# First graph attention of a two-layer kernel: the mask is brought into PSUM once for two heads, the odd head's logits come from a difference added to the same bank, and there are four logit buffers in place of three

## The chip, the cores and the metric

The program runs on one core of one Trainium2 chip. The metric is the device time of that core in microseconds, the median of several executions. The kernel before takes 2636.36 us (three runs, 2636.29 to 2637.47).

## What is computed

The whole program is two layers, each an attention over a graph of 2708 nodes with 256 features, followed by a feed-forward part. The change touches the first attention alone, whose reference is, cut to what matters:

```python
support = (inputs @ weight).reshape(n, H, OUT_F).transpose(1, 0, 2)      # H = 4 heads of 64
f1 = jnp.einsum('hno,ho->hn', support, weight_u[..., 0])
f2 = jnp.einsum('hno,ho->hn', support, weight_v[..., 0])
logits = f1[:, None, :] + f2[:, :, None]
w = jax.nn.leaky_relu(logits, NEG_SLOPE)
masked = w * adj_mat
mask = adj_mat != 0.0
neg = jnp.where(mask, masked, -jnp.inf)
m = jnp.max(neg, axis=2, keepdims=True)
e = jnp.where(mask, jnp.exp(neg - m), 0.0)
denom = jnp.sum(e, axis=2, keepdims=True)
out = jnp.einsum('hnm,hmo->hno', e / denom, support)
```

The rows of an output tile are 128 nodes, so there are 22 tiles; a row of logits has 2708 columns. The mask is the same for the four heads of a tile.

## The kernel before, in words

`layer0_attention` works in units. A unit is one tile and one head (22 x 4 = 88 units); a pair is the two units of heads 0 and 1, or 2 and 3, of one tile (44 pairs). In the names of the trace `a_` stands ahead of the tiles of this stage. The five engines run their own programs, written out without loops over the units by `over_units`, which calls a function `step` of each engine once per unit; the order within an engine is the order of the code, and semaphores tie the engines together. A unit "of an even head" is head 0 or 2.

A unit passes through these places:
- TensorE, `logits(unit, c)`: a row of logits comes in three chunks of 1024, 1024 and 660 columns. For each chunk, one of two PSUM slots `fo` gets the mask (OFF through the identity IDB, line 770) and then the logits (ROWS and FP, line 772), each as matmuls of at most 512 columns. It may write a slot when VectorE has read the chunk two places before (`leaky_done`).
- VectorE, `leaky(unit, c)` (line 683) makes the leaky value of a chunk out of `fo` into the logit buffer `lg`; `mask(unit)` (line 691) multiplies the whole row with ADJ and takes the maximum, and line 694 negates it.
- ScalarE, `exp_part(unit)` (line 626): the exponential of a whole row with its sum.
- TensorE, `turn` (line 785): 22 transposes of 128x128 blocks into three PSUM banks `tp`, four blocks to a bank, so six groups: groups 0 to 2 first and 3 to 5 (10 blocks) later in the step.
- ScalarE, `copies` (line 570): each group is copied from `tp` into `wt`. `copied` lets TensorE use the bank again.
- TensorE, `weighted(pair, half)` (line 800): the product with V, both heads of a pair side by side, in two halves of 11 blocks each, one half in each step of the pair two units later. `heads_in` is raised by the second half. `po` has one place for the sums, so half 0 waits for `heads_out` of the pair before.
- ScalarE, `sums_out` (line 634) copies the sums into `ot`; TensorE, `turn_back` (line 808), turns them; VectorE, `finish` (line 714), adds them to X and raises `heads_out`.

TensorE's step for a unit is: groups 0 to 2 of this unit, the third chunk of logits of the unit two later, groups 3 to 5, in a step of an even head `turn_back`, two chunks of logits of the unit three later, half of `weighted`. ScalarE's step is: copies of groups 0 to 2, in a step of an even head `sums_out` of the pair before last, the exponential of the next unit, copies of groups 3 to 5. VectorE's step is: three `leaky` of the unit two later, in a step of an even head `finish`, in one of head 3 `row_stats`, then `mask` of the unit two later, and in a step of an odd head `reciprocals`.

`copies` waits, besides for the transposes, for `heads_in` of the pair two before the unit's own, since `wt` holds two pairs:

```python
if first_of(unit).later(-4):
    eng.wait_ge(heads_in, pairs(first_of(unit).later(-4)))
copy(wt[:, h // 2, h % 2, j:end, :], tp[:, BANKS[g], 0:(end - j) * P]).then_inc(copied[BANKS[g]], 1)
```

(`later(k)` counts in units, so `later(-4)` of the first unit of a pair is the pair two before; `pairs` turns a pair into the count that its semaphore has.)

Of the kernel before, what the change touches and what calls it, by code (L numbers as in the profile page):

```python
# [5 lines left out]
ALU = mybir.AluOpType  # L6
# [8 lines left out]
P = 128  # L15
# [145 lines left out]
def layer0_prepare(nc, io, keep):  # L161
# [4 lines left out]
    with Phase(nc, "p0") as ph:  # L166
# [106 lines left out]
        def _(dve):  # L273
# [28 lines left out]
            def selectors():  # L302
# [6 lines left out]
                dve.wait_ge(sel_done, 3)  # L309
                for h in range(H):  # L310
                    dve.tensor_scalar(SEL[:, h, :], ones[:, :], hsel[:, h:h + 1], None, ALU.mult).then_inc(sel_done, 1)

            def first_rows(b):

                dve.wait_ge(sel_done, 3 + H)
                dve.tensor_copy(ROWS[:, b, :, :], SEL[:, :, :]).then_inc(sel_done, 1)
# [156 lines left out]
LB = 3  # L473
# [3 lines left out]
TB = 3  # L477
# [3 lines left out]
BANKS = [g % TB for g in range(NG)]  # L481


def layer0_attention(nc, io, keep):
# [6 lines left out]
    with Phase(nc, "a0") as ph:  # L491
# [6 lines left out]
        wt = ph.sb("wt", [P, HPAIR, 2, NT, P])  # L498
# [15 lines left out]
        (leaky_done, heads_in, ot_done, back, den_ok, rec_done, heads_out, x_stats, x_folded, x_moments,  # L514
         x_pchain) = ph.sems(
            "leaky_done heads_in ot_done back den_ok rec_done heads_out x_stats x_folded x_moments x_pchain")
# [19 lines left out]
        def chunk(unit, c):  # L536

            i, b, h = unit
            k = (b * H + h) * NC + c
            return k % 2, i * (H * NC) + (k // 2 + 1)  # L540

        def leaky_count(unit, c):

            i, b, h = unit
            return i * (2 * H * NC) + ((b * H + h) * NC + c + 1)
# [74 lines left out]
        def _(act):  # L620
# [25 lines left out]
            def step(unit):  # L646
# [3 lines left out]
                if unit[2] % 2 == 0 and unit.later(-4):  # L650
                    sums_out(unit.later(-4))
# [15 lines left out]
            sums_out(last_unit(0))  # L667
# [3 lines left out]
        def _(dve):  # L671
            def leaky(unit, c):
# [5 lines left out]
                if not unit.later(-H) and h == 0:  # L678
                    table_ready(dve, (c + 1) * per_chunk)
                elif not unit.later(-H) and c == 0:  # L680
                    table_ready(dve, (h + 1) * len(pieces))
# [42 lines left out]
            def step(unit):  # L724
                ahead = unit.later(2)
                if ahead:
                    leaky(ahead, 0)
                    leaky(ahead, 1)
                    leaky(ahead, 2)
                if unit[2] % 2 == 0 and unit.later(-4):  # L730
                    finish(unit.later(-4))
                if unit[2] == H - 1 and unit.later(-H - 1):
                    row_stats(unit.later(-H - 1))
                if ahead:
                    mask(ahead)
                if unit[2] % 2:
# [9 lines left out]
            for h in range(2):  # L746
                for c in range(NC):
                    leaky(Unit(0, 0, h, h), c)
                mask(Unit(0, 0, h, h))
# [3 lines left out]
            finish(last_unit(0))  # L753
# [3 lines left out]
        def _(pe):  # L757
            def logits(unit, c):
# [10 lines left out]
                for n0, nn in spans:  # L769
                    pe.matmul(fo[:, s, n0:n0 + nn], IDB[:, :], off[:, b, c0 + n0:c0 + n0 + nn], start=True, stop=False)  # L770
                for n0, nn in spans:
                    mm = pe.matmul(fo[:, s, n0:n0 + nn], ROWS[:, b, h, :], FP[:, c0 + n0:c0 + n0 + nn],  # L772
                                   start=False, stop=True)
# [15 lines left out]
            def weighted(unit, half):  # L789

                i, b, h0 = unit
                if half == 0:
                    if unit.later(-2):
                        pe.wait_ge(heads_out, pairs(unit.later(-2)))
                    for g in range(NG - TB, NG):
                        pe.wait_ge(copied[BANKS[g]], uses(unit.later(1), g))
                mid = NT // 2
                for j in range(*((0, mid) if half == 0 else (mid, NT))):
                    for s in range(2):
                        mm = pe.matmul(po[s * HD:(s + 1) * HD, 0:P], V[:, j, h0 + s, 0:HD], wt[:, h0 // 2, s, j, :],  # L800
                                       start=(j == 0), stop=(j == NT - 1))
                if half == 1:
                    mm.then_inc(heads_in, 1)
# [1718 lines left out]
```

## Time and profile before

| | |
|---|---|
| median of 3 runs | 2636.36 us |
| the profiled execution: its time, its span | 2640.07 us, 2638.4 us |
| busy share of the span: TensorE matmul, VectorE, ScalarE, GpSimd | 95%, 75%, 62%, 54% |
| the stage of the change | from about 72 us to 741 us of the span |
| the stage, matmul busy | 660.40 of 669.00 us |
| the stage, VectorE busy, ScalarE busy | 607.83 us, 515.74 us |

The shares of the whole span are means over stages with different limits. In this stage TensorE is busy nearly all the time, VectorE nine tenths of it. The trace shows a matmul that is pipelined with the next one as longer than the distance to the next start; so what a group of matmuls costs is read here from the start of the group to the start of the next.

### The profile page before, as it was taken

How to read it: one execution, taken by the hardware profiler on the slowest of the kernel's cores; microseconds unless marked ns; L12 is line 12 of the kernel's file. 1: busy time of each engine (PE TensorE's matmuls, PEld its weight loads, DVE VectorE, ACT ScalarE, POOL GpSimd, SP SyncE). 2: the span in 40 equal slices, each digit the busy share in tenths (PEclk: the TensorE clock that was granted, in tenths of full speed). 3: DMA queues.
4: the chain of work that ended last, by engine and by line, in shares of the span. 5: the costliest groups of instructions: out<-in, count | busy, mean ns of one | idle time of the engine just before them, and what ended most of it. 6: DMA issues, size and time to landing. Idle time of an engine off the chain costs nothing. (4 is left out here: it accounts for less than half of the span.)

```text
span 2638.4 us, 58062 instructions
## 1 busy us (share of the span) xinstructions
PE 2494.7 (95%) x20229; PEld 2033.1 (77%) x20230; DVE 1977.0 (75%) x4248; ACT 1641.0 (62%) x3123; POOL 1429.2 (54%) x1715
## 2 busy tenths in 40 slices
PE   7899999999967998679999999999799999999999
PEld 6577777777746997557777777777688888888888
DVE  5899999999944443887777777777677777777776
ACT  1777777777733333346666666666677777777775
POOL 8666666666343553622222222222478888888886
PEclk9999999999987999889999999999899999999999
DMA  2011111111064223201111111110000000000001
GB/s 102 23 65 44 44 44 45 63 44 44 23 227 147 72 70 108 86 7 44 45 54 49 42 42 42 42 42 22 7 1 0 0 0 0 0 0 0 0 0 42
DMA packets 43785, 114.03 MB, mean 43 GB/s; under 512 B 5542, under 2 KB 29839, under 8 KB 37903
## 3 DMA queue, kind: packets, MB, share of 16 engines
q1 hardware_dynamic: 38094, 97.16, 10.5%
q0 software_dynamic: 5568, 15.21, 1.9%
q8 instruction: 81, 1.33, 0.2%
q14 instruction: 42, 0.34, 0.0%
HBM read 99.20 MB, written 13.15 MB: 43 GB/s over the span
## 5 line engine op out<-in xcount | busy, mean ns | idle before, releaser
L2394 PE MATMUL f_pm<-f_wl,f_yt 128*128 128x256 f32 x2640 | 626.0, 381 | 0.0
L2394 PEld LDWEIGHTS f_pm<-f_wl,f_yt 128*128 128x128 f32 x2640 | 478.6, 191 | 52.2
L1139 POOL TENSOR_TENSOR ADJ<-ADJ,OFF 128x2708 f32<-128x2708 f32 x21 | 125.4, 5972 | 539.7 <-DVE ADJ L1220 539.7
L120 POOL TENSOR_SCALAR f_yy<-f_th,f_rs 128x255 f32<-128x255 f32 x660 | 370.2, 576 | 24.3 <-POOL f_rs L115 24.3
L2176 DVE SCALAR_TENSOR_TENSOR f_gg<-f_th,f_pm 128x512 f32<-128x512 f32 x319 | 219.0, 686 | 176.8 <-ACT f_th L2315 175.7
L570 ACT COPY a_wt<-a_tp 128x512 f32<-128x512 f32 x528 | 256.6, 566 | 144.2 <-PE a_tp L785 144.1
L683 DVE SCALAR_TENSOR_TENSOR a_lg<-a_f1s,F2S,a_fo 128x1024 f32<-128x1024 f32 (+1 forms) x264 | 296.5, 1152 | 31.8 <-PE a_fo L772 30.0
L598 POOL TENSOR_SCALAR OFF<-ADJ 128x677 bf16<-128x677 f32 x84 | 284.2, 3406 | 65.2 <-DMA ADJ<-in_adj 65.2
L1200 DVE CUSTOM_DVE_ANT_0 a_sc<-a_qk,ADJ 128x1024 f32<-128x1024 f32 (+1 forms) x264 | 288.3, 1093 | 34.2 <-PE a_qk L1310 34.2
L2315 ACT ACTIVATE f_th<-f_pm 128x512 f32<-128x512 f32 x319 | 190.7, 598 | 194.4 <-PE f_pm L2394 194.4
L1115 ACT COPY XF<-a_tp 128x512 f32<-128x512 f32 x264 | 154.3, 585 | 236.2 <-PE a_tp L1332 235.4
L1163 ACT ACTIVATE a_sc<-a_sc,a_mx 128x1024 f32<-128x1024 f32 (+1 forms) x264 | 277.7, 1052 | 35.2 <-DVE a_mx L1205 35.2
L691 DVE CUSTOM_DVE_ANT_0 a_lg<-a_lg,ADJ 128x2708 f32<-128x2708 f32 x88 | 261.4, 2971 | 1.2
L1332 PE MATMUL a_tp<-ident,a_sc 128*128 128x128 f32 x1936 | 261.7, 276 | 0.4 <-ACT XF L1115 0.2
L1332 PEld LDWEIGHTS a_tp<-ident,a_sc 128*128 128x128 f32 x1936 | 215.4, 141 | 42.4 <-issue 19.7
L2183 DVE BATCH_NORM_STATS2 f_st<-f_th 128x6 f32<-128x256 f32 x660 | 245.5, 415 | 0.5 <-ACT f_th L2319 0.5
L785 PE MATMUL a_tp<-ident,a_lg 128*128 128x128 f32 x1936 | 245.3, 275 | 0.6 <-ACT a_wt L570 0.6
L1353 PEld LDWEIGHTS a_po<-XF,V 128*64 128x64 f32 x3872 | 208.7, 137 | 41.5 <-issue 36.3
L1353 PE MATMUL a_po<-XF,V 128*64 128x128 f32 x3872 | 240.3, 276 | 0.0
L800 PEld LDWEIGHTS a_po<-a_wt,V 128*64 128x64 f32 x3872 | 209.6, 137 | 37.1 <-issue 35.5
L1115 DVE COPY XF<-a_tp 128x512 f32<-128x512 f32 (+1 forms) x264 | 158.3, 600 | 98.4 <-PE a_tp L1332 98.4
L800 PE MATMUL a_po<-a_wt,V 128*64 128x128 f32 x3872 | 230.6, 275 | 1.1 <-DVE X L714 1.1
(345 smaller groups left out, 4566.5 us busy)
## 6 DMA issues: line engine op xcount, KB each, us to landing
ADJ<-in_adj SPq DMA_DIRECT2D x44, 1354.0 KB, 5.9
W<-in_L_ffn_w SPq DMA_DIRECT2D x32, 512.0 KB, 9.7
out<-X SPq DMA_DIRECT2D x21, 128.0 KB
XD<-XF SPq DMA_DIRECT2D x3, 768.0 KB
m_b<-in_L_ffn_b SPq DMA_DIRECT2D x1, 2048.0 KB, 9.6
QT<-YD SPq DMA_DIRECT2D x2, 768.0 KB, 9.0
V<-YD SPq DMA_DIRECT2D x2, 768.0 KB, 10.6
X<-in_x SPq DMA_DIRECT2D x1, 1024.0 KB, 10.2
```

What stands on the lines that cost most here:

```text
L120: return eng.tensor_scalar(out, x, rs[:, 0, bass.ds(t, 1)], rs[:, 1, bass.ds(t, 1)], ALU.mult, ALU.add)
L570: copy(wt[:, h // 2, h % 2, j:end, :], tp[:, BANKS[g], 0:(end - j) * P]).then_inc(copied[BANKS[g]], 1)
L598: pool.tensor_scalar(off[:, b, cols], adj[:, b, cols], 0.0, HUGE, ALU.is_equal, ALU.mult).then_inc(off_done[b], 1)
L683: dve.scalar_tensor_tensor(lg[:, unit.turn, c0:c0 + cn], f1s[:, h, c0:c0 + cn], F2S[:, bass.ds(i * 2 + b, 1), h], fo[:, s, 0:cn], ALU.add, ...
L691: dve.tensor_tensor_reduce(lg[:, unit.turn, :], lg[:, unit.turn, :], adj[:, b, :], 1.0, FLOOR, ALU.mult, ALU.max, mx[:, h, 0:1]).then_inc( ...
L800: mm = pe.matmul(po[s * HD:(s + 1) * HD, 0:P], V[:, j, h0 + s, 0:HD], wt[:, h0 // 2, s, j, :], start=(j == 0), stop=(j == NT - 1))
L1115: copy(wt[:, (hp * NC + c) % 2, s, j - c * CT:end - c * CT, :], tp[:, bank(group), 0:(end - j) * P]).then_inc(copied[bank(group)], 1)
L1163: act.activation(sc[:, h, c0:c0 + cn], sc[:, h, c0:c0 + cn], ACT.Exp, bias=mx[:, h, NC:NC + 1], accum_out=den[:, h, c:c + 1]).then_inc(exp ...
L1200: dve.tensor_tensor_reduce(sc[:, h, c0:c0 + cn], qk[:, s, 0:cn], adj[:, b, c0:c0 + cn], 1.0, -BIG, ALU.add, ALU.max, mx[:, h, c:c + 1]).th ...
L1332: mm = pe.transpose(tp[:, bank(group), (j - j0) * P:(j - j0 + 1) * P], sc[:, h, col:col + P], ident[:, :])
L1353: mm = pe.matmul(po[s * HD:(s + 1) * HD, 0:P], V[:, j, 2 * hp + s, 0:HD], wt[:, (hp * NC + c) % 2, s, j - c * CT, :], start=(j == 0), stop ...
L2394: mm = pe.matmul(out, yt[:, g, r, k, :], wl[:, k, :], start=(k == 0), stop=(k == KD - 1))
```

## The change

The logits of a tile are made in a written order of head and chunk, `ORDER`. A chunk of an even head gets mask and logits as before. The chunk of the odd head of the same pair comes two places later, so in the same PSUM slot, and gets one set of matmuls alone: ROWS of an odd head now holds the difference to the even head, and it is added to what stands in the slot. `lg` has four buffers in place of three. `wt` is divided: `wt_head` for blocks 0 to 11 (groups 0 to 2) has one place for each of the two heads of a pair; `wt_tail` for blocks 12 to 21 has one for the odd heads and two for the even ones. `weighted` is cut at block 12, comes in the step after groups 0 to 2 instead of at its end, and its first half raises a semaphore of its own, `half_in`. `copies`, `sums_out`, `turn_back` and `finish` are rearranged to this.

```diff
-LB = 3
+LB = 4
+MID = 12
+ORDER = [(0, 0), (0, 1), (1, 0), (1, 1), (0, 2), (2, 0), (1, 2), (3, 0), (2, 1), (2, 2), (3, 1), (3, 2)]
+PLACES_OF = {hc: n for n, hc in enumerate(ORDER)}
...
-        wt = ph.sb("wt", [P, HPAIR, 2, NT, P])
+        wt_head = ph.sb("wth", [P, 2, MID, P])
+        wt_tail = ph.sb("wtt", [P, 1 + HPAIR, NT - MID, P])
...
+        def wt_part(h, j, end):
+
+            if end <= MID:
+                return wt_head[:, h % 2, j:end, :]
+            return wt_tail[:, 0 if h % 2 else 1 + h // 2, j - MID:end - MID, :]
...
                 eng.wait_ge(turned[BANKS[g]], uses(unit, g))
-                if first_of(unit).later(-4):
-                    eng.wait_ge(heads_in, pairs(first_of(unit).later(-4)))
-                copy(wt[:, h // 2, h % 2, j:end, :], tp[:, BANKS[g], 0:(end - j) * P]).then_inc(copied[BANKS[g]], 1)
+                before = first_of(unit).later(-2)
+                two_before = first_of(unit).later(-4)
+                if g < TB and before:
+                    eng.wait_ge(half_in, pairs(before))
+                elif h % 2 and before:
+                    eng.wait_ge(heads_in, pairs(before))
+                elif two_before:
+                    eng.wait_ge(heads_in, pairs(two_before))
+                copy(wt_part(h, j, end), tp[:, BANKS[g], 0:(end - j) * P]).then_inc(copied[BANKS[g]], 1)
...
(ScalarE)
                 copies(act, act.copy, unit, range(0, TB))
-                if unit[2] % 2 == 0 and unit.later(-4):
-                    sums_out(unit.later(-4))
+                if unit[2] % 2 and first_of(unit).later(-2):
+                    sums_out(first_of(unit).later(-2))
                 if unit.later(1):
                     exp_part(unit.later(1))
                 copies(act, act.copy, unit, range(TB, NG))
...
(VectorE)
                 ahead = unit.later(2)
-                if ahead:
-                    leaky(ahead, 0)
-                    leaky(ahead, 1)
-                    leaky(ahead, 2)
-                if unit[2] % 2 == 0 and unit.later(-4):
-                    finish(unit.later(-4))
+                first = 3 * number_of(unit) + 8
+                held = unit[2] == H - 1
+                for n in range(first, min(first + (2 if held else 3), OPS)):
+                    leaky(*logit_at(n))
                 if unit[2] == H - 1 and unit.later(-H - 1):
                     row_stats(unit.later(-H - 1))
                 if ahead:
                     mask(ahead)
+                if unit[2] % 2 and first_of(unit).later(-2):
+                    finish(first_of(unit).later(-2))
+                if held and first + 2 < OPS:
+                    leaky(*logit_at(first + 2))
...
(TensorE)
-                for n0, nn in spans:
-                    pe.matmul(fo[:, s, n0:n0 + nn], IDB[:, :], off[:, b, c0 + n0:c0 + n0 + nn], start=True, stop=False)
+                if h % 2 == 0:
+                    for n0, nn in spans:
+                        pe.matmul(fo[:, s, n0:n0 + nn], IDB[:, :], off[:, b, c0 + n0:c0 + n0 + nn],
+                                  start=True, stop=False)
...
                     if unit.later(-2):
                         pe.wait_ge(heads_out, pairs(unit.later(-2)))
-                    for g in range(NG - TB, NG):
-                        pe.wait_ge(copied[BANKS[g]], uses(unit.later(1), g))
-                mid = NT // 2
-                for j in range(*((0, mid) if half == 0 else (mid, NT))):
+                for g in (range(0, TB) if half == 0 else range(TB, NG)):
+                    pe.wait_ge(copied[BANKS[g]], uses(unit.later(1), g))
+                for j in range(*((0, MID) if half == 0 else (MID, NT))):
...
-                if half == 1:
-                    mm.then_inc(heads_in, 1)
+                mm.then_inc(heads_in if half else half_in, 1)
...
                 turn(unit, range(0, TB))
-                if unit.later(2):
-                    logits(unit.later(2), 2)
-                turn(unit, range(TB, NG))
-                if even and unit.later(-4):
-                    turn_back(unit.later(-4))
-                if unit.later(3):
-                    logits(unit.later(3), 0)
-                    logits(unit.later(3), 1)
+                first = 3 * number_of(unit) + 10
                 if first_of(unit).later(-2):
                     weighted(first_of(unit).later(-2), 0 if even else 1)
+                if first < OPS:
+                    logits(*logit_at(first))
+                turn(unit, range(TB, NG))
+                if not even and first_of(unit).later(-2):
+                    turn_back(first_of(unit).later(-2))
+                for n in (first + 1, first + 2):
+                    if n < OPS:
+                        logits(*logit_at(n))
```

The rows below are the order of TensorE's instructions for a step of head 2 and the first rows of the next, well inside the stage, first before the change. A row has the line, the operation, what it writes and reads, its size and how many stand in a row.

```order
L785 MATMUL a_tp<-ident,a_lg 128x128 x12
L770 MATMUL a_fo<-OFF,IDB 128x512
L770 MATMUL a_fo<-OFF,IDB 128x148
L772 MATMUL a_fo<-FP,ROWS 128x512
L772 MATMUL a_fo<-FP,ROWS 128x148
L785 MATMUL a_tp<-ident,a_lg 128x128 x10
L808 MATMUL a_po<-ident,a_ot 128x128
L770 MATMUL a_fo<-OFF,IDB 128x512 x2
```

After the change the same step stands so (`a_wth` is `wt_head`, `a_wtt` is `wt_tail`).

```order
L823 MATMUL a_tp<-ident,a_lg 128x128 x12
L837 MATMUL a_po<-a_wth,V 64x128 x24
L807 MATMUL a_fo<-OFF,IDB 128x512
L807 MATMUL a_fo<-OFF,IDB 128x148
L810 MATMUL a_fo<-FP,ROWS 128x512
L810 MATMUL a_fo<-FP,ROWS 128x148
L823 MATMUL a_tp<-ident,a_lg 128x128 x10
L807 MATMUL a_fo<-OFF,IDB 128x512 x2
L810 MATMUL a_fo<-FP,ROWS 128x512 x3
L810 MATMUL a_fo<-FP,ROWS 128x148
L823 MATMUL a_tp<-ident,a_lg 128x128 x12
L837 MATMUL a_po<-a_wtt,V 64x128 x20
```

The product with V moved from the end of the step to the place behind the first twelve transposes, with 24 and 20 matmuls in place of 22 and 22, and of the last chunks one is without OFF.

ScalarE's order in the two steps of a pair is, before the change:

```order
L570 COPY a_wt<-a_tp 128x512 x3
L634 COPY a_ot<-a_po 128x128
L626 ACTIVATE a_lg,a_den<-a_lg,a_mx 128x2708
L570 COPY a_wt<-a_tp 128x512 x2
L570 COPY a_wt<-a_tp 128x256
L570 COPY a_wt<-a_tp 128x512 x3
L626 ACTIVATE a_lg,a_den<-a_lg,a_mx 128x2708
```

And after it:

```order
L606 COPY a_wth<-a_tp 128x512 x3
L662 ACTIVATE a_lg,a_den<-a_lg,a_mx 128x2708
L606 COPY a_wtt<-a_tp 128x512 x2
L606 COPY a_wtt<-a_tp 128x256
L606 COPY a_wth<-a_tp 128x512 x3
L670 COPY a_ot<-a_po 128x128
L662 ACTIVATE a_lg,a_den<-a_lg,a_mx 128x2708
```

The copies and the exponentials keep their places; the copy of the sums moved from the first step of a pair to the second, and the copies of groups 0 to 2 go to the tile that has one place per head.

VectorE, in a step of head 3, has now this order: two chunks, the statistics, the mask, `finish`, and a chunk held back behind it.

```order
L716 SCALAR_TENSOR_TENSOR a_lg<-a_f1s,F2S,a_fo 128x1024
L716 SCALAR_TENSOR_TENSOR a_lg<-a_f1s,F2S,a_fo 128x660
L755 BN_STATS a_st<-X 128x6
L724 ISA a_lg,a_mx<-a_lg,ADJ 128x2708
L724 ISA a_mx 128x1
L727 TENSOR_SCALAR a_mx<-a_mx 128x1
L747 SCALAR_TENSOR_TENSOR X<-a_po,a_rec,X 128x64 x2
L716 SCALAR_TENSOR_TENSOR a_lg<-a_f1s,F2S,a_fo 128x1024
```

Before the change `finish` stood ahead of the mask in the steps of even heads, and all three chunks ahead of it.

## Rows read from the trace of the kernel before

**Rows 1.** Stretches of the stage: busy us of each engine (instructions), granted clock, DMA share, GB/s

```profile
72.00:741.00 669.00, 660.40 (x6845) 515.88 (x6847) 607.83 (x730) 515.74 (x852) 415.88 (x176) 1.00 0.12 43
402.27:417.18 14.91, 14.91 (x160) 11.77 (x158) 13.54 (x18) 12.12 (x21) 11.18 (x5) 1.00 0.22 85
417.18:432.07 14.89, 14.89 (x159) 11.76 (x158) 14.05 (x17) 10.96 (x17) 7.77 (x5) 1.00 0.05 8
```

**Rows 2.** Group by line and shape, 200 to 680 us: busy, mean ns | idle before

```profile
L570 ACT COPY a_wt<-a_tp 128x512 f32<-128x512 f32 x323 | 170.7, 597 | 108.7 <-PE a_tp L785 108.7
```

**Rows 3.** Timeline of TensorE, one pair: start, us, engine, line, names, count

```profile
402.27 1.53 PE L785 MATMUL a_tp<-ident,a_lg 128*128 128x128 f32 x12
403.64 0.45 PE L770 MATMUL a_fo<-OFF,IDB 128*128 128x512 bf16 x2
403.93 0.44 PE L772 MATMUL a_fo<-FP,ROWS 128*128 128x512 bf16 x2
404.20 1.25 PE L785 MATMUL a_tp<-ident,a_lg 128*128 128x128 f32 x10
405.29 0.27 PE L808 MATMUL a_po<-ident,a_ot 128*128 128x128 f32 x1
405.40 0.60 PE L770 MATMUL a_fo<-OFF,IDB 128*128 128x512 bf16 x2
405.84 0.59 PE L772 MATMUL a_fo<-FP,ROWS 128*128 128x512 bf16 x2
406.27 0.60 PE L770 MATMUL a_fo<-OFF,IDB 128*128 128x512 bf16 x2
...
407.23 2.62 PE L800 MATMUL a_po<-a_wt,V 128*64 128x128 f32 x44
409.78 1.53 PE L785 MATMUL a_tp<-ident,a_lg 128*128 128x128 f32 x12
```

**Rows 4.** Timeline of ScalarE in the first step of that pair

```profile
402.97 1.56 ACT L570 COPY a_wt<-a_tp 128x512 f32<-128x512 f32 x3 [2.05 <-PE a_tp L785]
404.41 0.29 ACT L634 COPY a_ot<-a_po 128x128 f32<-128x128 f32 x1
404.56 2.59 ACT L626 ACTIVATE a_lg<-a_lg,a_mx 128x2708 f32<-128x2708 f32 x1
...
407.11 1.37 ACT L570 COPY a_wt<-a_tp 128x512 f32<-128x512 f32 x3
```

**Rows 5.** Timeline of VectorE in that pair

```profile
404.40 0.90 DVE L683 SCALAR_TENSOR_TENSOR a_lg<-a_f1s,F2S,a_fo 128x660 f32<-128x660 f32 x1 [0.62 <-PE a_fo L772]
405.61 0.48 DVE L714 SCALAR_TENSOR_TENSOR X<-a_po,a_rec,X 128x64 f32<-128x64 f32 x2 [0.30 <-PE a_po L808]
406.00 2.97 DVE L691 CUSTOM_DVE_ANT_0 a_lg<-a_lg,ADJ 128x2708 f32<-128x2708 f32 x1
...
409.09 2.47 DVE L683 SCALAR_TENSOR_TENSOR a_lg<-a_f1s,F2S,a_fo 128x1024 f32<-128x1024 f32 x2
411.91 0.90 DVE L683 SCALAR_TENSOR_TENSOR a_lg<-a_f1s,F2S,a_fo 128x660 f32<-128x660 f32 x1 [0.34 <-PE a_fo L772]
412.73 0.42 DVE L722 BATCH_NORM_STATS2 a_st<-X 128x6 f32<-128x256 f32 x1
413.06 2.96 DVE L691 CUSTOM_DVE_ANT_0 a_lg<-a_lg,ADJ 128x2708 f32<-128x2708 f32 x1
```

**Rows 6.** Timeline at the stage's start, where TensorE's queue waits for a ScalarE copy

```profile
96.28 0.56 ACT L570 COPY a_wt<-a_tp 128x512 f32<-128x512 f32 x1
...
96.95 0.14 PEld L785 LDWEIGHTS a_tp<-ident,a_lg 128*128 128x128 f32 x1 [1.04 <-ACT a_lg L626]
```

**Rows 7.** Stretches of 4 us at the stage's start, columns as in rows 1

```profile
84.00:88.00 4.00, 1.46 (x6) 0.29 (x3) 3.97 (x3) 4.00 (x6) 4.00 (x2) 1.00 0.00 0
88.00:92.00 4.00, 3.93 (x14) 2.20 (x15) 2.45 (x5) 2.44 (x8) 2.60 (x1) 0.59 0.00 0
104.00:108.00 4.00, 2.19 (x17) 1.70 (x18) 3.79 (x9) 4.00 (x6) 2.92 (x2) 1.00 0.65 227
```

More of the change, by code:

```diff
@@ L313, in first_rows @@
             def first_rows(b):
-                dve.wait_ge(sel_done, 3 + H)
-                dve.tensor_copy(ROWS[:, b, :, :], SEL[:, :, :]).then_inc(sel_done, 1)
+                dve.wait_ge(sel_done, 4 + H)
+                dve.tensor_copy(ROWS[:, b, 0:H:2, :], SEL[:, 0:H:2, :])
+                dve.tensor_tensor(ROWS[:, b, 1:H:2, :], SEL[:, 1:H:2, :], SEL[:, 0:H:2, :],
+                                  ALU.subtract).then_inc(sel_done, 1)
             def results(i, b):
@@ L481, with logit_place, logit_at @@
 BANKS = [g % TB for g in range(NG)]
+ORDER = [(0, 0), (0, 1), (1, 0), (1, 1), (0, 2), (2, 0), (1, 2), (3, 0), (2, 1), (2, 2), (3, 1), (3, 2)]
+PLACES_OF = {hc: n for n, hc in enumerate(ORDER)}
+OPS = NT * H * NC
+def logit_place(unit, c):
+    i, b, h = unit
+    return (i * 2 + b) * H * NC + PLACES_OF[(h, c)]
+def logit_at(n):
+    tile, k = divmod(n, H * NC)
+    h, c = ORDER[k]
+    return Unit(tile // 2, tile % 2, h, tile * H + h), c
 def layer0_attention(nc, io, keep):
@@ L513, in layer0_attention @@
         turned, copied = (ph.sems(" ".join(f"{n}{k}" for k in range(TB))) for n in ("turned", "copied"))
-        (leaky_done, heads_in, ot_done, back, den_ok, rec_done, heads_out, x_stats, x_folded, x_moments,
+        (leaky_done, half_in, heads_in, ot_done, back, den_ok, rec_done, heads_out, x_stats, x_folded, x_moments,
          x_pchain) = ph.sems(
-            "leaky_done heads_in ot_done back den_ok rec_done heads_out x_stats x_folded x_moments x_pchain")
+            "leaky_done half_in heads_in ot_done back den_ok rec_done heads_out x_stats x_folded x_moments x_pchain")
         block = ph.block()
@@ L536, in chunk, with leaky_count, number_of @@
         def chunk(unit, c):
-            i, b, h = unit
[L539 to L545, printed above, removed]
+            n = logit_place(unit, c)
+            return n % 2, n // 2 + 1
+        def leaky_count(unit, c):
+            return logit_place(unit, c) + 1
+        def number_of(unit):
+            i, b, h = unit
+            return (i * 2 + b) * H + h
         def uses(unit, g):
@@ L666, in _ @@
             over_units(act, step)
-            sums_out(last_unit(0))
             sums_out(last_unit(H - 2))
@@ L677, in leaky @@
                     dve.wait_ge(turned[BANKS[NG - 1]], uses(unit.later(-LB), NG - 1))
[L678 to L681, printed above, removed]
+                if not unit.later(-H):
+                    table_ready(dve, h * len(pieces) + (c + 1) * per_chunk)
                 dve.wait_ge(fo_done[s], number)
@@ L745, in _ @@
             table(0, len(pieces) // 2)
[L746 to L749, printed above, removed]
+            for n in range(8):
+                leaky(*logit_at(n))
+                if n == PLACES_OF[(0, NC - 1)]:
+                    mask(Unit(0, 0, 0, 0))
+                elif n == PLACES_OF[(1, NC - 1)]:
+                    mask(Unit(0, 0, 1, 1))
             over_units(dve, step)
@@ L830, in table @@
                               start=True, stop=True).then_inc(spread[n % TB], 1)
-            for c in range(NC):
-                table(c * per_chunk, (c + 1) * per_chunk)
-                logits(Unit(0, 0, 0, 0), c)
-            table(len(pieces), 2 * len(pieces))
-            for c in range(NC):
-                logits(Unit(0, 0, 1, 1), c)
-                if c == 1:
-                    table(2 * len(pieces), 3 * len(pieces))
-            table(3 * len(pieces), H * len(pieces))
-            for c in range(2):
-                logits(Unit(0, 0, 2, 2), c)
+            made = 0
+            for n in range(10):
+                unit, c = logit_at(n)
+                end = max(made, unit[2] * len(pieces) + (c + 1) * per_chunk)
+                table(made, end)
+                made = end
+                logits(unit, c)
+            table(made, H * len(pieces))
             table_ready(pe, H * len(pieces))
             over_units(pe, step)
-            turn_back(last_unit(0))
             weighted(last_unit(H - 2), 0)
```

6 lines of the change are left out of this document (3 added, 3 removed).

## The prediction, made before the changed kernel was run

> **What bounds the kernel now.** I looked first at the stretches of the stage. TensorE is busy for 660.40 of its 669.00 us and for all of each of the two pairs of a tile (14.91 and 14.89 us, so 29.80 us per tile) [rows 1]. VectorE is busy for 13.54 and 14.05 us of them, close behind, ScalarE for 12.12 and 10.96 [rows 1]. So TensorE sets the pace, and less work for it can give little before VectorE stops it. Next I read the timelines of the three engines over one pair, to see not how busy they are but who waits, and how long before he is needed each one is done. ScalarE waits for transposes, in total 108.7 us over 65 units [rows 2], 2.05 us ahead of the first copy in the pair shown [rows 4]. This is its slack, and it is all that stands between ScalarE's chain and TensorE: TensorE's step begins at 402.27, ScalarE starts its copy behind the exponential at 407.11 and TensorE wants that bank at 409.78 [rows 3, 4]. With 0.60 us for a copy [rows 2] and 0.11 us until TensorE's queue goes on (96.28 + 0.56 to 96.95, [rows 6]) that chain is ready 5.55 us into a step of 7.51 us. The slack is 1.96 us.
>
> **What the change takes away.** Per pair three chunks lose the mask matmuls: five of 512 columns and one of 148. Two of 512 take 0.44 us from start to start (405.40 to 405.84, and 405.84 to 406.27 for the next two), and 512 and 148 together 0.29 (403.64 to 403.93) [rows 3]. That is 0.43 + 0.43 + 0.29 = 1.15 us per pair, and TensorE would need 13.75 us per pair.
>
> A page of the Trainium skill prices the same instructions lower: "TensorE: Matmul & The Clock Gate", section "Back-to-back issue gap", gives about 131 ns for a matmul of 512 columns in a sustained stream. The trace shows 216 to 220 ns, so it doesn't agree here. By the page's figure the five large ones are worth an estimated 0.66 us per pair instead of 1.08; the sum below goes by the trace.
>
> **What it adds: ScalarE's copies of groups 0 to 2 now wait for TensorE.** `wt_head` has one place per head, and the pair before is still in it. It is read out by `weighted(..., 0)`, which stands in TensorE's step of the same even head, behind the first twelve transposes. So in each even step the three copies can't start until that half is over, and behind them on ScalarE are queued the exponential of the next unit and the copies of groups 3 to 5; TensorE's next step needs both. In each odd step `sums_out` now waits for the second half, made in the same step, and the same exponential and copies stand behind it. Before, neither waited: the copies start 0.70 us into the step (402.97) and the sums were long ready.
>
> I work the steps through with these durations, all from start to start: 12 transposes 1.37 us, 10 transposes 1.09, a chunk with mask 0.87 (405.40 to 406.27), an odd one 0.43, a short one 0.56 or 0.27, the product for 11 blocks 2.55 (407.23 to 409.78), so 2.78 for 12 and 2.32 for 10; a group's last matmul record ends 0.07 (product) or about 0.16 (logits) behind the next start [rows 3]. Three copies 1.44, the sums 0.15, from the exponential to the copy behind it 2.55 [rows 4]. VectorE: a chunk 1.24 (half of 2.47), a short one 0.82, mask with what hangs on it 3.09 (406.00 to 409.09), `finish` 0.39 to the next start and 0.48 to its end, statistics 0.33 [rows 5]. An engine starts 0.03 us after the end of a matmul record (403.93 + 0.44 to 404.40, [rows 3, 5]). What VectorE needs to release TensorE isn't shown; it lies between 0.03 and 0.11, and I take 0.11, the one of ScalarE, since the side that waits is the same.
>
> Step of head 0, counted from its start: transposes to 1.37, half 0 to 4.15, its last record ends at 4.22, copies from 4.25 to 5.69, exponential to 8.24, first copy done 8.84, TensorE goes on at **8.95**. TensorE's own work in it is over by about 7.2.
>
> Step of head 1, from its start: 1.37, half 1 to 3.69, `sums_out` from 3.79, exponential from 3.94, copy from 6.49, done 7.09, next step at **7.20**. In the same step the chunk behind the product is chunk 1 of the next tile's head 0, with mask: to 4.56, record to 4.72, VectorE from 4.75 to 5.99, mask to 9.08, and then `finish`, which ends at 9.56 and which TensorE's next half 0 waits for (`heads_out`), so until 9.67.
>
> Step of head 2, on the same count: starts at 7.20, its transposes are done at 8.57, so TensorE waits 1.10 us. Half 0 to 12.45, copies from 12.55, exponential from 13.99, copy from 16.54, done 17.14, next step at 17.25, **10.05** us after the start. VectorE gets the next short chunk (12.45 + 0.56 + 0.17) at 13.21, mask from 14.03 to 17.12.
>
> Step of head 3: VectorE goes on with 1.24 + 0.82 + 0.33 to 19.51 and the mask to 22.60, `finish` after `turn_back` (17.25 + 1.37 + 2.32 + 0.43 + 1.09 + 0.27 = 22.73) to 23.15, then the chunk held back to 24.39. TensorE's last chunk of the step waits for it (`leaky_done`) until 24.50 and takes 0.56: next tile at 25.06, **7.81** us. ScalarE's chain would have been there at 24.45.
>
> A tile is 8.95 + 7.20 + 10.05 + 7.81 = 34.01 us against 29.80, so 4.21 us more. 43 of the 44 pairs have a pair before them, 21.5 tiles: 4.21 x 21.5 = 90.5 us. The fourth logit buffer, the order of chunks and the two small subtractions ahead of the stage I cost at nothing: the first lets VectorE run ahead, which it can't use here as it waits for `fo`; the last are single instructions in a stage that begins at 72 us. Without cover they would cost under 1 us.
>
> The profiled execution took 2640.07 us, 3.7 more than the median of the runs; this sum makes it 2730.6, and the median 2636.4 + 90.5 = **2727**.
>
> **The rivals.**
> *ScalarE's chain alone.* If VectorE is early enough with `finish` and the held chunk, only the first two steps' lengths count: 8.95 + 7.20 = 16.15 against 14.90 per pair, 1.25 x 43 = 54, so 2690. For it: VectorE has less to do than TensorE takes. Against: its third chunk of each step now comes behind the product and the mask behind that.
>
> *Gain.* The copies are not held, because the half is read in time. It decides at the slack: a copy of an even step must start within 0.70 + 1.96 = 2.66 us of its step, where I find 4.25. If so, TensorE needs 13.75 us and VectorE is busy for (13.54 + 14.05) / 2 = 13.80 [rows 1], so 1.10 us less for each of 43 pairs, 47 us, and the time is 2589. Against it speaks the written order alone, and that is plain. By the page's 131 ns the gain would be an estimated 0.7 us per pair, 30 us.
>
> *The clock.* At the stage's start TensorE was busy for 1.46 of 4 us and the granted clock of the next 4 us was 0.59, so some 3.3 us of them at 1.2 GHz in place of 2.4; where it was busy for 2.19 of 4 us the clock stayed at 1.00 [rows 7]. In the step of head 2 it would wait 1.1 and then nearly 2 us. If the clock fell once per tile, 3.3 us at half speed would cost up to 1.6 us, 35 us in all: 2762.
>
> **How the numbers follow.** The forecast 0.62, with 2708 to 2745 as its own range (a releaser of 0.03 instead of 0.11 us takes 4 to 6 us away, more from what hides; an added 0.1 us at each of about eight waits per tile adds 17); ScalarE's chain alone 0.20; the clock 0.06; the gain 0.08; no change, where the waits eat just what is freed, 0.04. The range 2686 to 2748 takes in the first two. About 0.2% is what a measurement of this kernel can tell from no change. Slower by more than that: 0.62 + 0.20 + 0.06 and half of the last, 0.90; faster 0.08; the same 0.02.
>
> **What the profile after would show.** Right: the lines of the stage with ScalarE idle ahead of its copies and released by the product with V, some 3 to 5 us in each even step; TensorE no longer always busy but idle ahead of the transposes, with the copy as the releaser, some 1.7 us in even steps; idle ahead of the product behind `finish` once per tile; VectorE idle ahead of its third chunk, 2 to 3 us; the mask matmuls halved to 264; the stage some 90 us longer, all else as it was. Wrong: a period per tile under 29.8 us, or ScalarE's first copy within 2.7 us of the start of its step. Steps of about 9 and 7.2 us in turn, with no idle time behind `finish`, would speak for the first rival; a clock under 1.00 in the middle of the stage for the third.

## The result, and the profile after

The changed kernel takes 2747.51 us (median of 4 runs, 2747.44 to 2748.95) against 2636.36: ratio 1.0421, 95% interval 1.0408 to 1.0434. It is slower, 111 us by the medians and 107.3 us by the spans of the profiled executions (2745.7 and 2638.4 us). The forecast was 2727, 90.5 us slower, with 2708 to 2745 as its own range and 2686 to 2748 as the whole one. So the measured time lies 2.5 us above the forecast's own range and only 0.5 us inside the whole one.

The stretches of the stage in the changed kernel, columns as in [rows 1]; the second row is one tile, from a first step to the next:

```profile
72.00:849.00 777.00, 619.38 (x6452) 486.13 (x6537) 631.21 (x720) 519.28 (x848) 387.09 (x171) 0.99 0.10 37
401.56:436.31 34.75, 27.97 (x300) 22.18 (x303) 28.87 (x34) 23.27 (x39) 17.53 (x9) 1.00 0.12 41
```

A tile takes 34.75 us where it took 29.80 [rows 1]. TensorE, busy all the time before, is busy for 27.97 of them. 4.95 x 21.5 tiles is 106.4 us, so the whole loss lies in the stage's steady state.

Its chain of waits, from 60 to 860 us: who waited for whom, us in total, times, longest.

```profile
ACT a_wth L606 <- PE a_po L837: 172.4, 43, 4.7
...
DVE a_lg L716 <- PE a_fo L810: 119.5, 43, 5.0
PEld a_tp L823 <- ACT a_lg L662: 108.6, 66, 2.9
PE a_tp L823 <- ACT a_wtt L606: 81.8, 66, 2.7
ACT a_ot L670 <- PE a_po L837: 76.9, 44, 5.0
```

The first row is the new wait: in 43 even steps ScalarE's copies into `wt_head` are held by the product. TensorE's waits for ScalarE ahead of the transposes (108.6 and 81.8 us) hang on it: in the experiment e1 below, where the first row is gone, they are 21.4 and 11.5 us. The two others come from the product's new place: VectorE waits for the chunk and ScalarE for the sums behind it, in e1 still for 107.4 and 76.1 us. The timeline of TensorE over that tile, where [rows 3] showed no idle time:

```profile
401.56 1.47 PE L823 MATMUL a_tp<-ident,a_lg 128*128 128x128 f32 x12
402.96 2.84 PE L837 MATMUL a_po<-a_wth,V 128*64 128x128 f32 x48
...
410.75 1.50 PE L823 MATMUL a_tp<-ident,a_lg 128*128 128x128 f32 x12 [1.65 <-ACT a_wtt L606]
412.19 2.40 PE L837 MATMUL a_po<-a_wtt,V 128*64 128x128 f32 x40
...
418.06 1.50 PE L823 MATMUL a_tp<-ident,a_lg 128*128 128x128 f32 x12 [0.44 <-ACT a_wtt L606]
420.42 2.84 PE L837 MATMUL a_po<-a_wth,V 128*64 128x128 f32 x48 [0.85 <-DVE X L747]
...
428.08 1.50 PE L823 MATMUL a_tp<-ident,a_lg 128*128 128x128 f32 x12 [1.52 <-ACT a_wtt L606]
...
435.74 0.45 PE L807 MATMUL a_fo<-OFF,IDB 128*128 128x512 bf16 x2 [1.22 <-DVE a_lg L716]
...
436.31 1.47 PE L823 MATMUL a_tp<-ident,a_lg 128*128 128x128 f32 x12
```

The four steps start at 401.56, 410.75, 418.06 and 428.08: 9.19, 7.31, 10.02 and 8.23 us. And ScalarE in the first of them, which answers to [rows 4]:

```profile
405.90 1.57 ACT L606 COPY a_wth<-a_tp 128x512 f32<-128x512 f32 x3 [3.36 <-PE a_po L837]
407.50 2.55 ACT L662 ACTIVATE a_lg<-a_lg,a_mx 128x2708 f32<-128x2708 f32 x1
...
410.05 1.33 ACT L606 COPY a_wtt<-a_tp 128x512 f32<-128x512 f32 x3
```

The copies start 4.34 us into the step instead of 0.70; the first copy behind the exponential starts at 8.49 instead of 4.84, and TensorE goes on as soon as it is done.

### The profile page after: what moved, and what is told of

The parts are those of the page before. It is cut to its first block and busy times, and to the rows that moved or that the text cites. A ratio compares the mean times of both kernels' runs of the same rounds, so it can differ in the third digit from the quotient of the medians.

```text
span 2745.7 us, 57516 instructions
## 1 busy us (share of the span) xinstructions
PE 2449.9 (89%) x19879; PEld 2000.9 (73%) x19966; DVE 2012.5 (73%) x4251; ACT 1646.0 (60%) x3123; POOL 1403.1 (51%) x1715
## 5 line engine op out<-in xcount | busy, mean ns | idle before, releaser
L823 PE MATMUL a_tp<-ident,a_lg 128*128 128x128 f32 x1936 | 248.9, 278 | 93.3 <-ACT a_wtt L606 81.8
L823 PEld LDWEIGHTS a_tp<-ident,a_lg 128*128 128x128 f32 x1936 | 213.3, 142 | 151.8 <-ACT a_lg L662 108.6
L634 POOL TENSOR_SCALAR OFF<-ADJ 128x677 bf16<-128x677 f32 x84 | 261.0, 3130 | 69.3 <-DMA ADJ<-in_adj 69.3
L724 DVE CUSTOM_DVE_ANT_0 a_lg<-a_lg,ADJ 128x2708 f32<-128x2708 f32 x88 | 271.1, 3081 | 3.3 <-DVE a_lg L716 0.2
L642 POOL TENSOR_TENSOR ADJ<-ADJ,OFF 128x677 f32<-128x677 f32 x84 | 122.7, 1483 | 276.8 <-issue 143.5
L606 ACT COPY a_wth<-a_tp 128x512 f32<-128x512 f32 x264 | 138.4, 595 | 176.8 <-PE a_po L837 172.4
```

Source lines behind the costliest of these rows:

```text
L634: pool.tensor_scalar(off[:, b, cols], adj[:, b, cols], 0.0, HUGE, ALU.is_equal, ALU.mult).then_inc(off_done[b], 1)
L724: dve.tensor_tensor_reduce(lg[:, unit.turn, :], lg[:, unit.turn, :], adj[:, b, :], 1.0, FLOOR, ALU.mult, ALU.max, mx[:, h, 0:1]).then_inc( ...
L823: mm = pe.transpose(tp[:, BANKS[g], (j - j0) * P:(j - j0 + 1) * P], lg[:, unit.turn, col:col + P], ident[:, :])
```

## Experiments

Each kernel is the changed one with the edit shown. Ratios are to the kernel before, run on the same chip; the intervals are of 95%. The kernel before took from 2636.36 to 2638.64 us (medians) beside the changed kernel and the ten edits, so a difference between medians of two kernels can be off by some 2 us.

**e1, two places for even heads.**

```diff
-        wt_head = ph.sb("wth", [P, 2, MID, P])
+        wt_head = ph.sb("wth", [P, 3, MID, P])
...
-                return wt_head[:, h % 2, j:end, :]
+                return wt_head[:, 2 if h % 2 else h // 2, j:end, :]
...
-                if g < TB and before:
+                if g < TB and h % 2 and before:
                     eng.wait_ge(half_in, pairs(before))
+                elif g < TB and not h % 2 and two_before:
+                    eng.wait_ge(half_in, pairs(two_before))
```

> The early blocks of even heads get two places, so ScalarE's copies of groups 0 to 2 of an even head no longer wait for the product's first half of the same step. My theory (the single place for even heads holds ScalarE and through it TensorE): the copies start some 0.7 us into an even step again instead of 4.3, ScalarE's idle time released by the product ahead of its copies (172 us now) goes to near zero, and the even steps lose their idle time of about 1.6 us ahead of the next transposes. What stays is the chain product, third chunk, mask, finish or held chunk on VectorE, which by the rows of the changed kernel ends 1.2 and 0.85 us late once per tile each, so not all of 2 x 1.6 x 21.5 = 69 us comes back: about 40 us, 2707. Rival (VectorE's late third chunk alone sets the pace, the hold of ScalarE is hidden behind it): within 10 us of 2747.

Measured: 2727.08 us, ratio 1.0339 (1.0322 to 1.0356): 20 us back where 40 were expected. The wait of the copies for the product is gone, so the hold was real. But TensorE's idle time gathered in one place. TensorE at the end of the tile:

```profile
425.72 0.59 PE L812 MATMUL a_fo<-FP,ROWS 128*128 128x512 bf16 x2
429.65 0.73 PE L809 MATMUL a_fo<-OFF,IDB 128*128 128x512 bf16 x2 [3.34 <-DVE a_lg L718]
430.18 0.76 PE L812 MATMUL a_fo<-FP,ROWS 128*128 128x512 bf16 x2
430.73 2.46 PE L825 MATMUL a_tp<-ident,a_lg 128*128 128x128 f32 x12
433.13 2.84 PE L839 MATMUL a_po<-a_wth,V 128*64 128x128 f32 x48
```

and the stretches around it, columns as in [rows 1]:

```profile
401.00:426.00 25.00, 23.61 (x254) 18.79 (x250) 22.58 (x24) 17.56 (x27) 11.00 (x6) 1.00 0.16 57
426.00:434.00 8.00, 4.66 (x34) 3.63 (x34) 6.29 (x10) 4.95 (x13) 6.59 (x3) 0.79 0.01 2
```

After an idle stretch of 3.34 us the granted clock was 0.79 in the mean over 8 us, so 3.4 us of them at 1.2 GHz and the rest at 2.4. Twelve transposes took 2.40 us from start to start (430.73 to 433.13), before and after elsewhere 1.40. The mean from 120 to 730 us is 0.95, where the changed kernel has 1.00.

**e2, the step's first chunk ahead of the product.**

```diff
-                if first_of(unit).later(-2):
-                    weighted(first_of(unit).later(-2), 0 if even else 1)
                 if first < OPS:
                     logits(*logit_at(first))
+                if first_of(unit).later(-2):
+                    weighted(first_of(unit).later(-2), 0 if even else 1)
```

> TensorE makes the step's first chunk of logits ahead of the product instead of behind it; the single place for even heads stays. My theory: VectorE gets its third chunk 2.3 to 2.8 us earlier, but the half that ScalarE waits for ends 0.4 to 0.9 us later, and ScalarE's chain sets the step, so the kernel gets slower, by 0.4 to 0.9 us in each of about 86 steps less what VectorE gives back once per tile: some 10 to 20 us, about 2762. Rival (VectorE's late third chunk sets the pace): faster by 1.2 + 0.85 us per tile or more, 40 us or more, 2705.

Measured: 2770.86 us, ratio 1.0503 (1.0486 to 1.0521), 23 us slower than the changed kernel, where 10 to 20 were expected. VectorE's third chunk comes earlier and the kernel gets slower. The four steps of a tile take 9.62, 8.18, 9.82 and 7.96 us instead of 9.19, 7.31, 10.02 and 8.23: the chunks that now stand ahead of the product in the first two (0.43 and 0.87 us) count in full, and the last two steps give back 0.47. The rival that VectorE's late chunk alone sets the pace falls.

**e3, both edits.** The edit is that of e1 and that of e2.

> Both edits of the two kernels before. My theory: each of the two chains is broken, and only then does the kernel come near the time before the change: about 7.5 us per step, 94 us less, 2653. If the two effects simply added up, it would be the sum of the two single results (about 2722 by my numbers). Rival (ScalarE's chain alone): as the first kernel.

Measured: 2651.77 us, ratio 1.0052 (1.0035 to 1.0069). Singly the edits give -20 and +23 us, together -96, so they don't add up. TensorE waits for two chains side by side: when ScalarE's alone is cut short, it waits for VectorE's (3.34 us in e1), and when VectorE's chunk alone comes earlier, ScalarE still holds it. The second edit is worth 75 us once the first has been made. By e6 below some 26 of them are the clock, which was 1.00 in the mean from 120 to 730 us in this kernel and 0.95 in e1.

**e4, the exponential ahead of the early copies in even steps.**

```diff
+                if unit.later(1) and unit[2] % 2 == 0:
+                    exp_part(unit.later(1))
                 copies(act, act.copy, unit, range(0, TB))
...
-                if unit.later(1):
+                if unit.later(1) and unit[2] % 2:
                     exp_part(unit.later(1))
```

> ScalarE makes the exponential ahead of the copies of groups 0 to 2 in steps of even heads; the single place stays, so the copies wait as long, but nothing of 2.55 us is queued behind them. My theory: the even step loses most of its idle time ahead of the next transposes, since the first later copy comes about 2.5 us sooner; TensorE then is held behind groups 0 to 2 (their copies start at 4.3 us or, if the exponential is late, later) and by VectorE's chain: 35 us less, 2712. Rival (the wait itself, not what stands behind it): no change, 2747.

Measured: 2739.96 us, ratio 1.0392 (1.0375 to 1.0409), 8 us back of the 35. The direction is that of the theory, the size isn't: once more TensorE stands 2.93 us for VectorE's held chunk once per tile, and the clock was 0.95 in the mean over 120 to 730 us, as in e1. In e1 such a fall cost 26 us (see e6), which is about what is missing here; no run tested that for e4.

**e5, the mask matmuls of the odd heads put back.**

```diff
-                if h % 2 == 0:
-                    for n0, nn in spans:
+                for n0, nn in spans:
...
-                dve.tensor_tensor(HSEL[:, 1:H:2], HSEL[:, 1:H:2], HSEL[:, 0:H:2], ALU.subtract).then_inc(sel_done, 1)
```

(and `first_rows` as it was before the change).

> The changed kernel with the one part undone that its name speaks of: odd heads get mask and whole logits again, as before (two matmuls more per chunk, ROWS without differences); order, buffers and places as changed. My theory (the product's new place and the single place for even heads cost the time, the removed matmuls are worth nothing while TensorE waits): 1.15 us of matmuls per pair return, most of it into idle time, except in the step of head 3, where an odd chunk lies ahead of VectorE's held chunk: up to 0.4 us per tile, so 0 to 10 us slower, 2752. Rival (TensorE's work still counts): 43 x 1.15 = 50 us slower, 2797.

Measured: 2751.51 us, ratio 1.0430 (1.0413 to 1.0448), 4 us slower than the changed kernel by the medians, 2 by the ratios, whose intervals overlap. In the traces a tile takes 34.86 us here and 34.75 in the changed kernel, which makes 2.4 us in 21.5 tiles. What the change is named after is worth 2 to 4 us here, hardly more than nothing: TensorE's idle stretches shrink instead (1.65 to 1.37 us, 1.52 to 1.25, 1.22 to 0.90). The loss comes from the order, buffers and places that go with it.

**e6, e1 with filler.** Sixteen transposes of the identity into columns of `po` that nobody reads; they are added work and change no output.

```diff
                 pe.wait_ge(ot_done, pairs(unit))
+                for _ in range(16 if unit[2] == 0 else 0):
+                    pe.transpose(po[:, 3 * P:4 * P], ident[:, :], ident[:, :])
                 pe.transpose(po[:, P:2 * P], ot[:, :], ident[:, :]).then_inc(back, 1)
```

> The kernel with two places for even heads, and 16 transposes of the identity into unused columns of po, whose result nobody reads, ahead of turn_back in each step of head 3. They take 1.7 us of TensorE inside the 3.3 us in which it waited once per tile for VectorE, after which the granted clock fell to 1.2 GHz for 3.4 us. My theory (that fall took back half of what the two places gave): the clock stays at 1.00 and about 1.2 us per tile come back (12 transposes 1.4 instead of 2.4 us, a chunk 0.85 instead of 1.08), some 25 us less than the kernel with two places: 2702. Rival (the wait alone costs, not the clock): 2727 or, if the added work is not hidden, more.

Measured: 2700.62 us, ratio 1.0238 (1.0221 to 1.0255). More work makes it 26 us faster than e1. TensorE over the same place:

```profile
412.79 1.91 PE L847 MATMUL a_po<-ident 128*128 128x128 f32 x16
...
417.26 0.45 PE L809 MATMUL a_fo<-OFF,IDB 128*128 128x512 bf16 x2 [1.59 <-DVE a_lg L718]
417.56 0.44 PE L812 MATMUL a_fo<-FP,ROWS 128*128 128x512 bf16 x2
417.83 1.47 PE L825 MATMUL a_tp<-ident,a_lg 128*128 128x128 f32 x12
```

The idle stretch is 1.59 us, the granted clock stays at 1.00 (also in the mean from 120 to 730 us), the twelve transposes take 1.41 us again (417.83 to 419.24), and the chunk ahead of them 0.57 (417.26 to 417.83) where e1 took 1.08; the 0.85 of the expectation was too high. So e1's gain without the clock is 47 us, and the fall took back 26.

**e7, a better order.** The edit of e1; the first chunk ahead of the product except in steps of head 3; the last chunk of a step of head 3 behind the next step's first transposes; `sums_out` behind the exponential.

```diff
+                ahead = unit[2] in (0, 1, 2)
+                if (unit[2] - 1) % H in (3,) and unit.later(-1) and first - 1 < OPS:
+                    logits(*logit_at(first - 1))
+                if ahead and first < OPS:
+                    logits(*logit_at(first))
...
-                if first < OPS:
+                if not ahead and first < OPS:
                     logits(*logit_at(first))
...
-                for n in (first + 1, first + 2):
+                for n in (first + 1, first + 2)[:1 if unit[2] in (3,) else 2]:
```

> Two places for even heads; the step's first chunk ahead of the product (not in a step of head 3); the last chunk of a step of head 3 moved behind the next step's first transposes, so that TensorE does not wait for VectorE's held chunk; ScalarE makes the exponential ahead of the copy of the sums. My theory: what is left in the kernel with both edits is one wait of 0.9 us of TensorE for VectorE's held chunk and one of 1.3 us for ScalarE behind the sums; both are covered now, and the period is set by VectorE: 28.5 to 30 us per tile, 2620 to 2650. Rival (VectorE is already the bound with both edits, since its small TENSOR_SCALAR of line 733 has grown from 0.32 to 0.7 us): no better than 2652.

Measured: 2648.25 us, ratio 1.0032 (1.0018 to 1.0046), 4 us less than e3, with intervals that overlap. The expected range held it, but the rival was nearly right: VectorE is busy for 574.53 of the 610 us from 120 to 730, TensorE for 557.70, and e9 below shows that time taken from VectorE comes off the whole.

**e8, another form of the small maximum.**

```diff
-                dve.tensor_scalar(rec[:, 0, two], den[:, two], 1e-30, None, ALU.max).then_inc(den_ok, 1)
+                dve.scalar_tensor_tensor(rec[:, 0, two], den[:, two], 1e-30, den[:, two], ALU.max, ALU.max).then_inc(den_ok, 1)
```

> As the kernel before it, with the maximum of the denominators made by SCALAR_TENSOR_TENSOR instead of TENSOR_SCALAR. In the changed kernel that TENSOR_SCALAR of 2 columns takes 0.84 us in the mean (0.32 before the change) and ends when the GpSimd operation on ADJ that runs beside it ends. Theory: it is this form that waits for GpSimd, the other does not: it takes 0.2 us, VectorE gets 0.5 us per pair back, 10 to 22 us less than the kernel before it, below the time before the change: about 2625. Rival (the wait is for the exponential or for any operation): the same duration and time as the kernel before it.

Measured: 2639.42 us, ratio 1.0003 (0.9993 to 1.0013), 9 us less than e7. In steps of head 1 the theory on the form falls: the operation still takes 1.12 us. The first row below is such a step, the second one of head 3:

```profile
407.44 1.12 DVE L737 SCALAR_TENSOR_TENSOR a_rec<-a_den 128x2 f32<-128x2 f32 x1
...
422.91 0.16 DVE L737 SCALAR_TENSOR_TENSOR a_rec<-a_den 128x2 f32<-128x2 f32 x1
```

GpSimd at both moments:

```profile
407.07 2.92 POOL L644 TENSOR_TENSOR ADJ<-ADJ,OFF 128x677 f32<-128x677 f32 x2 [4.38 <-issue]
...
419.87 3.52 POOL L636 TENSOR_SCALAR OFF<-ADJ 128x677 bf16<-128x677 f32 x1
```

Two elements per partition take 1.12 us when the operation starts inside GpSimd's first TENSOR_TENSOR (407.07 to about 408.55) and end with it. In the step of head 3 it takes 0.16, though GpSimd's operation on OFF is running (419.87 to 423.39). There the form does matter: in e7, at the same place and beside the same GpSimd operation, TENSOR_SCALAR takes 0.50 us in 19 tiles and 0.30 in one, and this form 0.15 to 0.16 in all of them. That is some 0.34 x 20, so 7 of the 9 us. So beside TENSOR_TENSOR on ADJ both forms are held, beside TENSOR_SCALAR on OFF only the TENSOR_SCALAR form.

**e9, the small operations ahead of the mask.** e7 with this:

```diff
+                if unit[2] == 1:
+                    reciprocals(first_of(unit))
                 if ahead:
                     mask(ahead)
...
-                if unit[2] % 2:
+                if unit[2] == H - 1:
                     reciprocals(first_of(unit))
```

> The kernel e7 (TENSOR_SCALAR as in the change) with VectorE's two small operations on the denominators moved, in steps of head 1, from behind finish to ahead of the mask. Behind finish they start while GpSimd's TENSOR_TENSOR on ADJ, which the same mask releases, is running, and end some 20 ns after it, 1.12 us later; ahead of the mask GpSimd's operations are over (402.7 against 404.0 in e8). Theory: what the operation waits for is GpSimd, not its own form and not the exponential: it takes 0.16 us there, and 0.96 us per tile come back, 21 us less than e8's 2639 at most, since VectorE sets the pace now: 2618 to 2628. Rival (it waits for something of its own unit): it stays at 0.6 us or more in the mean, and the time at 2639 or above.

Measured: 2626.63 us (5 runs, 2624.93 to 2628.80), ratio 0.9960 (0.9947 to 0.9974): 10 us faster than the kernel before and 121 faster than the changed one. Against e7, from which it differs by this move alone, it is 22 us, and the operation takes 0.16 us in steps of head 1 instead of 1.13, which makes 19 us in 20 tiles. The group of line 735 in e9: busy, mean ns, idle before.

```profile
L735 DVE TENSOR_SCALAR a_rec<-a_den 128x2 f32<-128x2 f32 x44 | 13.7, 311 | 0.0
```

In the changed kernel it was

```profile
L733 DVE TENSOR_SCALAR a_rec<-a_den 128x2 f32<-128x2 f32 x43 | 35.9, 835 | 0.0
```

so the changed kernel spent 22 us more of VectorE's time on these waits. In steps of head 3 it still takes 0.50 us in e9, and ends with the GpSimd operation on OFF beside it:

```profile
416.66 0.50 DVE L735 TENSOR_SCALAR a_rec<-a_den 128x2 f32<-128x2 f32 x1
```

```profile
413.62 3.52 POOL L636 TENSOR_SCALAR OFF<-ADJ 128x677 bf16<-128x677 f32 x1
```

The form of e8 took 0.16 there. The two were not put together in one kernel; from the 0.34 us per tile of e8, an estimate is another 7 us.

**e10, e9 with the mask matmuls put back.** The edit is that of e5.

> As e9, with the mask matmuls of the odd heads and their whole logits back. Theory: what the removed matmuls are worth depends on whether TensorE is waited for; in e5 they were worth 4 us, here, with both chains of waits covered, TensorE would need 14.9 us per pair again and more for its waits: 25 to 50 us slower than e9, 2650 to 2665. Rival (VectorE alone sets the pace now): under 10 us slower than e9.

Measured: 2659.74 us, ratio 1.0087 (1.0073 to 1.0100), 33 us slower than e9. The same matmuls that were worth 2 to 4 us in e5 are worth 33 here.

## Why the prediction was right, and where it was short

The direction and the chain of waits were forecast as they came. Of the 111 us 90.5 were forecast. That the measured time lies inside the whole range, by 0.5 us, is luck: its upper bound is only 3 us above that of the forecast's own range, which it missed, and no term of the sum stands for these 3 us. In the sum itself one start is written as 12.45 + 0.56 + 0.17, which is 13.18, where 13.21 is used; the 0.03 us for an engine's start is left out of the terms, not of the result.

- **The hold of ScalarE.** Right. Forecast for the step of head 0: copies from 4.25 us, TensorE's next step at 8.95; measured 4.34 and 9.19. e1 took this wait alone away, and by e6 it is worth 47 us. Of the 0.24 us of difference 0.16 are the three copies, which took 1.60 us to the exponential's start (405.90 to 407.50) and not 1.44.
- **The second half and the sums.** 7.20 forecast, 7.31 measured.
- **`finish` behind the mask.** 10.05 us forecast for the step of head 2, 10.02 measured, with 0.85 us idle ahead of the product, released by line 747.
- **VectorE's held chunk.** The mechanism was right (TensorE idle for 1.22 us at 435.74, released by VectorE), but the term was mis-sized: 7.81 us forecast, 8.23 measured. The mask of that step took 3.44 us where [rows 5] gave 2.97, and it began 0.20 us later than forecast, since the mask ahead of it began 1.05 us after the start of its short chunk (423.97 to 425.01) where the sum had 0.82. The step grew by 0.42 and not by more, because the wait for `turn_back` that the sum had here didn't come and VectorE released TensorE within 0.06 us instead of 0.11. In the changed kernel 20 of the 88 masks are that long, once per tile, and 0.47 x 20 is 9.4 us. I took VectorE's durations from a trace in which they didn't meet GpSimd at that moment.
- **The sum.** 4.21 us per tile forecast, 4.95 measured: 90.5 us against 106.4. The four steps make the difference: 0.24, 0.11, -0.03 and 0.42 us, so the mis-sized term is in the main the mask of the last one. The rest up to 111 us is between span and median: the profiled execution before was 3.7 us over its median, the one after is at it.
- **The worth of the removed matmuls.** I put 1.15 us per pair on TensorE's side and nothing in the sum. e5 shows 2 to 4 us. e10 against e9 gives 33 us of the 49 that 1.15 x 43 makes, where VectorE takes part of what TensorE gains. The Trainium skill, page "TensorE: Matmul & The Clock Gate", section "Back-to-back issue gap", prices a matmul of 512 columns at 131 ns, so the five large ones of a pair at an estimated 28 us in 43 pairs; the trace's 216 ns make 46. e10 doesn't decide between them; the distance from start to start in the traces does (405.40 to 405.84 for two, [rows 3]), and there the skill's figure doesn't hold.
- **The rivals.** "ScalarE's chain alone" (2690) fell: the waits behind `finish` and the held chunk are there. "The gain" (2589) fell; e9 shows that a gain can be had, 10 us, with other buffers and another order. "The clock" didn't happen in the changed kernel: it was 1.00 in the mean from 120 to 730 us, and no idle stretch there was over 1.65 us. It happened in e1 and e4, behind idle stretches of 3.34 and 2.93 us.

Open is why four edits of e7 gave no more: what each of them does alone beyond those of e1 and e2 wasn't run.

## What to carry to other kernels

A saving on the busiest engine is worth only what the next chain leaves: read for each other engine how long before it is needed it is ready, and compare that slack (1.96 us here) with what the buffers that pay for the saving will hold it up. When a buffer loses its second place, everything queued behind the waiting instruction on its engine is held as well; e1 cost 6 KB per partition and made the other edits worth making. And remove waits together, since one alone may only gather the idle time in one place, where the clock takes part of the gain back (26 of 47 us in e1).

## What the runs showed of the hardware

- **The clock takes back part of a removed wait.** Once per tile, 3.34 us idle in e1 was followed by 3.4 us at 1.2 GHz; with 2.93 us in e4 the mean clock was as low (0.95 from 120 to 730 us); 1.59 us in e6 and 1.65 us in the changed kernel were not followed by a fall. Added work that nobody needs was worth 26 us.
- **A small VectorE operation can last as long as a GpSimd operation.** 0.16 us alone, 1.12 us when it starts inside GpSimd's TENSOR_TENSOR, and in the changed kernel as in e8 it ended within 0.03 us of that one's end. The row of the operation holds the wait; no idle time is shown ahead of it. The Trainium skill, page "SBUF — State Buffer", section "SBUF: two separate sides", says that the two engines share a pair of ports and that the later one is blocked until the first is over, if the VectorE operation is in a 2-port mode, or has two inputs in SBUF while GpSimd's reads SBUF. The form of e8 has two such inputs. Beside TENSOR_TENSOR on ADJ (1.12 us) the trace agrees with that rule, beside TENSOR_SCALAR on OFF, which reads ADJ (0.16 us), it doesn't.
- **The mask is only partly held.** It has two inputs in SBUF, too. Started 0.14 us after the start of a GpSimd operation on OFF it took 3.44 us, started 1.76 us after it (the kernel before) 2.96, and it never waited for the end of an operation of 2.48 us. In the changed kernel VectorE and GpSimd:

```profile
430.46 3.44 DVE L724 CUSTOM_DVE_ANT_0 a_lg<-a_lg,ADJ 128x2708 f32<-128x2708 f32 x1
```

```profile
430.32 2.48 POOL L634 TENSOR_SCALAR OFF<-ADJ 128x677 bf16<-128x677 f32 x1
```

```
start after GpSimd's start (ns)   mask (ns)   kernel
 34                               3541        e2
137                               3439        changed
447                               3132        e5
659                               2965        e8
1761                              2960        before
```

  Start and duration add up to 3575, 3576 and 3579 ns in the first three rows, so the mask seems to begin its work only some 0.6 us after GpSimd's start. The twelve traces bear it out: in all of the 106 masks that start 0.02 to 0.58 us after such an operation the two add up to 3574 to 3581 ns, and the 146 that start 0.63 to 2.4 us after it take 2959 to 2980. Why the hold ends there no run shows. It doesn't fit the full block that the Trainium skill states on the page just named; the measurement decides.
- **GpSimd is held for the whole of a mask.** In 492 of 494 cases in the same traces an operation on OFF that began during a mask ended 2.34 to 2.36 us after the mask's end, whenever it began, and so lasted up to 5.3 us instead of 2.48. In the changed kernel the one ahead of the row above took 3.36 us (426.99 to 430.35) and ended 2.36 us after a mask (427.99). So it also depends on masks when GpSimd's next operation starts, and with it which mask is held: in e2, e3 and e7 to e9 one mask of 88 is long, in the changed kernel 20.
